# A decoder layer's loop over token chunks, written out as straight code on all five engines

## What is computed

```python
x = x + attn(layernorm(x), Wq, Wk, Wv, Wf, g_norm_w, Wo)      # gated slot attention, 4 heads, 64 slots
x = x + xattn(layernorm(x), ctx, ctx, W_q, W_k, W_v, W_o, ...) # 16 heads on 64 context rows, position bias
x = x + ffn(layernorm(x), Wr, W1, W3, W2)                      # 8 experts, top 2, capacity 1280, F = 1024
```

## Time and profile before

| | before |
|---|---|
| median of 3 runs | 1486.77 us (1482.56 to 1491.43) |
| profiled execution | 1484.94 us |
| its span, first to last instruction | 1482.9 us |
| mean granted TensorE clock | 0.972 of full speed |
| busy: TensorE / VectorE / ScalarE / GpSimd | 92% / 64% / 43% / 23% |
| the chunks, to chunk 31's score matmul | up to 709.51 us |
| instructions in the profile | 32499 |

### The profile page before, as it was taken

The page is one execution under the profiler, slowest core; times in us unless marked ns, Lnnn a source line. Parts: engine busy times, 40 slices in busy tenths (PEclk is TensorE's granted clock), DMA queues, the critical chain, the costliest instruction groups (busy, mean ns, idle before and its releaser), DMA issues. The chain is left out here.

```text
span 1482.9 us, 32499 instructions
## 1 busy us (share of the span) xinstructions
PE 1366.7 (92%) x10841; PEld 1214.5 (82%) x10841; DVE 951.4 (64%) x3162; ACT 633.6 (43%) x1596; POOL 346.0 (23%) x524
## 2 busy tenths in 40 slices
PE   6899999899999999999848999999999999999995
PEld 4677777777777767767628999999999999999995
DVE  5577888787887778778654556455554545555442
ACT  2444554454554444444324435344443434444331
POOL 3113232231231322222220222122211112121122
PEclk9999999999999999999858999999999999999998
DMA  3821210100100100000003242412424142231111
GB/s 92 232 80 32 96 52 18 31 30 17 31 31 16 31 26 20 31 30 13 22 28 115 40 116 33 115 30 52 104 33 116 30 114 39 68 82 30 30 23 22
DMA packets 67292, 79.67 MB, mean 54 GB/s; under 512 B 11090, under 2 KB 60723, under 8 KB 67154
## 3 DMA queue, kind: packets, MB, share of 16 engines
q1 hardware_dynamic: 52562, 59.09, 13.1%
q0 software_dynamic: 14592, 18.91, 7.7%
HBM read 44.04 MB, written 33.96 MB: 53 GB/s over the span
## 5 line engine op out<-in xcount | busy, mean ns | idle before, releaser
L862 ACT ACTIVATE h_a<-banks 128x256 f32<-128x256 f32 x320 | 122.5, 383 | 358.0 <-PE banks L1370 355.7
L1304 DVE TENSOR_TENSOR h_f<-banks,h_a 128x256 f32<-128x256 f32 x320 | 135.6, 424 | 158.9 <-ACT h_a L862 150.2
L506 POOL TENSOR_TENSOR idle_g<-half 128x1 f32<-128x1 f32 x144 | 29.3, 203 | 703.4 <-DVE y_s L1323 396.8
L1370 PE MATMUL banks<-xe_t_hi,w_even_hi 128*128 128x256 f32 x640 | 180.3, 282 | 0.1
L1370 PE MATMUL banks<-xe_t_hi,w_odd_hi 128*128 128x256 f32 x640 | 179.3, 280 | 0.0
L1370 PE MATMUL banks<-xe_t_lo,w_even_hi 128*128 128x256 f32 x640 | 178.4, 279 | 0.0
L1370 PE MATMUL banks<-xe_t_hi,w_even_lo 128*128 128x256 f32 x640 | 178.2, 279 | 0.0
L1370 PE MATMUL banks<-xe_t_lo,w_odd_hi 128*128 128x256 f32 x640 | 177.7, 278 | 0.0
L1370 PE MATMUL banks<-xe_t_hi,w_odd_lo 128*128 128x256 f32 x640 | 177.7, 278 | 0.0
L851 ACT ACTIVATE h_t_hi<-h_f 128x256 fp32r<-128x256 f32 x320 | 131.8, 412 | 32.0 <-DVE h_f L1304 31.8
L1311 DVE TENSOR_TENSOR h_t_lo<-h_f,h_t_hi 128x256 fp32r<-128x256 f32 x320 | 133.5, 417 | 6.1 <-ACT h_t_hi L851 5.3
(11 more groups left out here) (240 smaller groups left out, 3500.2 us busy)
## 6 DMA issues: line engine op xcount, KB each, us to landing
raw<-in_w SPq DMA_DIRECT2D x24, 1024.0 KB, 5.9
expert_rows<-empty SPq DMA_DIRECT2D x4, 2580.0 KB, 11.1
xe<-expert_rows SPq DMA_DIRECT2D x40, 258.0 KB, 2.8
xin<-in_x SPq DMA_DIRECT2D x32, 128.0 KB, 2.3
out_dram<-x SPq DMA_DIRECT2D x32, 128.0 KB, 1.9
out_dram<-y_s,token POOLq DMA_INDIRECT x80, 3.8
mask_i<-in_mask SPq DMA_DIRECT2D x32, 32.0 KB, 1.8
expert_rows<-r_xn,send POOLq DMA_INDIRECT x64, 3.1
```

The costliest lines, as they stand in the source:

```text
L506: return pool.tensor_tensor(idle_g[:, i:i + 1], half[:, 0:1], half[:, 0:1], ALU.add)
L862: act.activation(h_a[:, f % 2, :], bank[2 + f % 4][:, 0:GS], ACT.Silu).then_inc(silu_ok, 1)
L1304: dve.tensor_tensor(h_f[:, f % 2, :], bank[2 + f % 4][:, GS:2 * GS], h_a[:, f % 2, :], ALU.mult)\
L1370: last = pe.matmul(dst, lhs, rhs, start=(i == 0), stop=(i == len(pairs) - 1))
```

## The change

`over_chunks` no longer writes a loop: all 32 chunks are straight code on TensorE, VectorE, ScalarE and GpSimd, with plain numbers. SyncE's loop is written out in the same manner. The experts' loop `over_groups` stays as it is.

```diff
-        def over_chunks(eng, step, behind=None):
+        def over_chunks(step, behind=None):
             def at(b, c):
                 def run(lag, work):
                     n = b * CPB + c - lag
-                    if not isinstance(n, int) or 0 <= n < NCH:
+                    if 0 <= n < NCH:
                         work(n, (c - lag) % CPB, b + (c - lag) // CPB)
                 return run
-            for c in range(2 * CPB):
-                step(at(c // CPB, c % CPB))
-            with eng.Fori(2, B) as b:
-                for c in range(CPB):
-                    step(at(b, c))
+            for s in range(NCH):
+                step(at(s // CPB, s % CPB))
             for c in range(LAGS):
                 step(at(B, c))
...
             load_expert(0)
-            with sp.Fori(2, B - 1) as b:
-                for c in range(CPB):
-                    step(b, c)
-            for c in range(CPB):
-                step(B - 1, c, c < CPB - 1)
+            for s in range(2 * CPB, NCH):
+                step(s // CPB, s % CPB, s < NCH - 1)
...
-            over_chunks(pool, step)
+            over_chunks(step)
...
-            over_chunks(act, step, behind)
+            over_chunks(step, behind)
...
-            over_chunks(dve, step, behind)
+            over_chunks(step, behind)
...
-            over_chunks(pe, step)
+            over_chunks(step)
```

## The result

| | before | after |
|---|---|---|
| median of 7 runs | 1486.91 us (1482.56 to 1492.22) | 1473.74 us (1468.88 to 1481.46) |
| ratio after / before | | 0.9904, 95% interval 0.9876 to 0.9931 |
| profiled execution; its span | 1484.94 us; 1482.9 us | 1473.74 us; 1472.0 us |
| chunk 7's marker | 177.33 us | 182.97 us |
| from there to chunk 31's marker | 532.18 us | 521.50 us |

The forecast was 1476.2 us, 0.7% faster; measured is 1.0% faster, with an interval that just takes in 0.7%. All ratios here are estimates from fast runs and not quotients of two medians, so the two differ a little. The last four rows of the table split the two profiled executions. The stretch that the change touches became 10.7 us shorter. Beside it two parts with the same work moved in opposite directions, by +5.6 and -6.5 us; the experiments come back to both.

What follows compares the result with a forecast made beforehand. TensorE, 92% busy, was taken as the bound, idling at jumps because VectorE starts late. Jumps 11.17 us less waits 0.45 and 0.12 gave 10.6 us, taking the median from 1486.77 to 1476.2 us; range 1470.5 to 1483.

Steps and rivals of the forecast that it cites:

- chunk 31's marker: TensorE's first score matmul of chunk 31; as a sign of the forecast it was to come near 699 us.
- The jumps: Chunk loop's five jumps, each delaying VectorE's first instruction 2.3 to 2.6 us; writing them out was to gain 11.2 us.
- The added waits: TensorE's extra waits for banks in straight chunks: 0.44 us per three chunks, 0.45 and 0.12 us against the gain.
- The spells of the lower clock: Two spells of lower TensorE clock in the fourth and fifth looped stretches, counted as gone: 1.9 of the 11.2 us.
- Code to be fetched: Instruction fetch for 20 more chunk bodies: 24 more packets in the larger queue, about 90 in all, priced at nothing.
- The slower rival: TensorE's code fetch becomes the bound, each of 29 packets stopping it 2.3 us: about 1543 us; chance 0.07.
- the stall isn't the jump's: Rival: VectorE's 2.3 us pause stays in straight code, about 1487 us; chance 0.17 with a partial form at 1481.5.
- The sum: Net gain in the chunk 7 to 31 stretch: 11.17 - 0.45 - 0.12 = 10.6 us.
- The expert stage after chunk 31 lasts as long as before: Sign: the experts' stage, its loop and 1.7 us jump kept, was to stay unchanged in length.

Runs made afterwards that it cites:

- e2: Kernel before with only VectorE's chunk loop written out, the other engines keeping theirs: chunk 7 to 31 stretch 519.19 us, median 1471.31 us, ratio 0.9859.
- e4: All chunks straight except on VectorE, which keeps its loop: stretch 538.16 us, median 1491.51 us, ratio 1.0004 to the kernel before.
- e6: Changed kernel plus an eight-pass loop of one memset and one wait on VectorE ahead of chunk 16: 0.48 us a pass, stretch 526.10 us.
- e7: Kernel before with a twelve-chunk loop body run twice, SyncE's loop written out: stretch 526.11 us, median 1478.68 us, ratio 0.9944.
- e3: Changed kernel with one bank wait per tile in chunks 8 to 31, 28 a chunk instead of 104: stretch 518.01 us, ratio 0.9900 to the kernel before.
- e5: Kernel before profiled again, no edit: stretch 534.33 us, start up to chunk 7's marker 187.1 us, one timed run 1498.15 us.
- e1: Changed kernel run again, no edit: stretch 521.69 us, median 1476.49 us, ratio 0.9922 to the kernel before.
- e8: Straight chunks with the short list of waits (e3), experts' loop written out too: stretch 518.26 us, median 1471.00 us, ratio 0.9897 to the kernel before.
- e10: The e8 kernel timed again, no edit: stretch 518.22 us, median 1467.16 us, ratio 0.9836 to the kernel before.
- e9: Kernel before with VectorE's chunk loop and the experts' loop written out, other engines' chunk loops kept: stretch 517.91 us, median 1471.22 us, ratio 0.9867.
- e11: Changed kernel with one unused tile of 4 bytes per partition ahead of the others: stretch 521.42 us, one timed run 1489.25 us.

## Why the prediction was right, point by point

**The jumps.** Right in place and size. Five stretches were to go from 445.82 to 434.65 us; after, the five from 204.26 to 638.78 take 434.52. e2 and e4 show that VectorE's late start carries the cost, and e6 that it is the far target and not the branch, which the prediction had only argued. That no other engine's jump counts holds for the four-chunk body only: in e7 TensorE's own jump stopped it for 4.05 us.

**The added waits.** Right. 0.57 us was put against the gain (measured: 65.69 - 65.13 = 0.56 for the last three chunks and 21.29 - 21.23 = 0.06 for the interval into chunk 8), and 3.4 us over all 24 chunks as the difference to a kernel without them; e3 measured 3.5.

**The spells of the lower clock.** They are gone, as counted. That a jump's idle time causes each isn't shown: e2 has two with no wait for `f_st`. They occur in runs that kept some loop (two to four in those with the loop of before on VectorE), and in none of the stretches of the six profiles with all engines' chunks straight and nothing inserted.

**Code to be fetched.** Right: some 24 packets more were estimated and a little above 90 in all; it is 95, three of them for the added waits (92 in e3), which also shows that the queue is TensorE's, an "if" in the prediction. No stop of TensorE on "issue" is above 0.25 us in the stretch. The slower rival, TensorE stopped at each packet, didn't come, and neither did "the stall isn't the jump's".

**The sum.** 10.6 us for the stretch; measured 10.7 on the first pair of profiles (12.6 with the second pair, e5 and e1, whose before has four spells of the lower clock instead of two). The agreement to 0.1 us is thus in part luck; the second pair is 2 us off. The medians show 13.2 us and, in e1, 12.2.

**What it had wrong.** "The expert stage after chunk 31 lasts as long as before" failed by 6.5 us, one of the signs by which the prediction was to be wrong, and chunk 31's marker came at 704.5, not near 699. The second is the start, which e5 shows to vary by more than that with the same code. The first is the term that the sum lacked: ten groups of 17.4 us in before, none in after. In e5 and e2 there were nine, in e1, e3, e4 and e7 four or fewer (each of these has the experts' loop), in e8 to e10, without it, none. The three profiles with nine or ten are the ones whose TensorE runs both the four-chunk loop and the experts' loop, and in each they lie behind the experts' jump, most of them every second group. It hangs on more than chance, then, but not simply on TensorE's chunk loop, for e7 kept one of twelve chunks and had one slow group, and e9 kept the one of before and had none. e11 shows that the tiles' addresses can bring such groups; before and after share all addresses, so these can't be the difference between them. A dependence on where the code lies would fit and wasn't tried. How much of the 2.5 us between 10.7 and the medians' 13.2 is this stays open.

## What to carry to other kernels

Before costing a hardware loop, look at the first instruction of its body on the engine that leads the chunk: an "issue" wait that comes once per pass is the price of the jump (here 2.3 to 2.6 us on VectorE), and it counts only where the engine that bounds the time comes to wait for it; in e2 the jumps that were left cost nothing that could be seen. Writing out that one engine's loop can be enough, and a longer body isn't a cheaper one for each jump if TensorE no longer holds it from pass to pass. When a loop is written out, check which branches of the program's own helpers change with it, as the list of waits did here.

## What I had not expected of the hardware

One jump of a twelve-chunk body cost 8.4 us, against 2.3 to 3.4 for each jump of a four-chunk body: 4.05 us of TensorE on "issue", and some 10 us at half the clock that began in this idle time. And a shift of all tiles by 4 bytes made 25 of 38 intervals between expert groups 3.7% longer at full clock, with the stage 16.4 us longer in all, which no wait in the profile shows.
